# A message stage in which TensorE gathers two of every eight tiles by one-hot matrices

## The reference, cut to what matters

```python
h = jnp.maximum(_layernorm(x, axis=-1), 0.0)
edge_in = jnp.concatenate([edge_attr_64, h[src]], axis=1)    # 103125 x 128
msg = jax.nn.relu(edge_in @ W1 + b1)                         # 103125 x 64
msg_sum = jax.ops.segment_sum(msg, dst, num_segments=3125)
cnt = jax.ops.segment_sum(ones, dst, num_segments=3125)
reduced = msg_sum / jnp.maximum(cnt, 1.0)[:, None]
x = x + jax.nn.relu(jnp.concatenate([reduced, h], axis=1) @ W2 + b2)
```

## Time and profile before

| | us |
|---|---|
| median of three executions | 4684.26 |
| the profiled execution | 4702.03 |
| its span, first to last instruction | 4700.2 |
| first and last addition of the message stage (line 1640) | 3343.0 and 4599.1 |
| POOL busy / PE busy over the whole span | 1601.2 / 3335.4 |
| busy in line 1593, the gathers of this stage, 806 of them | 760.6 |

### The profile page before, as it was taken

How to read it: one execution, slowest core, us unless ns; L and a number is a source line. 1 busy time by engine, 2 the same in 40 slices (tenths; PEclk the granted TensorE clock), 3 DMA queues, 4 the chain that set the end, 5 groups by cost and what they waited for, 6 DMA issues and landing times. The chain is left out here.

```text
span 4700.2 us, 76229 instructions
## 1 busy us (share of the span) xinstructions
PE 3335.4 (71%) x17068; PEld 2240.2 (48%) x17068; DVE 1890.1 (40%) x6431; ACT 1176.8 (25%) x2939; POOL 1601.2 (34%) x1778
## 2 busy tenths in 40 slices
PE   1888787899979993777777777776455555555557
PEld 1444444455533332565566655665444444444445
DVE  4666665566620004444444444455222222222223
ACT  0566666000000001333333333343101010010100
POOL 3000000000000002566565556620366656566660
PEclk6988988899989996778777777787555555555555
DMA  0111111133367762222222222210111111111110
GB/s 26 57 59 57 59 59 59 50 105 88 115 225 286 287 230 51 56 54 54 52 54 53 53 53 54 54 45 12 34 42 44 43 43 43 42 44 42 43 43 11
DMA packets 418837, 338.43 MB, mean 72 GB/s; under 512 B 175992, under 2 KB 392088, under 8 KB 418488
## 3 DMA queue, kind: packets, MB, share of 16 engines
q1 hardware_dynamic: 362536, 277.79, 19.1%
q0 software_dynamic: 52736, 55.42, 6.0%
q10 hardware_dynamic: 3216, 0.82, 0.1%
HBM read 287.96 MB, written 45.86 MB: 71 GB/s over the span
## 5 line engine op out<-in xcount | busy, mean ns | idle before, releaser
L1593 POOL DMA_INDIRECT big<-message_table,src x806 | 760.6, 944 | 721.8 <-DVE big L1640 275.4
L1330 POOL DMA_INDIRECT big<-row_table,src x806 | 760.5, 944 | 565.1 <-issue 181.6
L1607 PE MATMUL banks<-big 64*128 64x64 f32 x1612 | 446.7, 430 | 213.2 <-DVE big L1640 196.7
L1616 PE MATMUL banks<-big 128*64 x1804 | 322.6, 328 | 384.2 <-issue 376.1
L1355 PE MATMUL banks<-big 97*128 x902 | 405.8, 541 | 153.0 <-issue 131.5
L1607 PEld LDWEIGHTS banks<-big 64*128 64x128 f32 x1612 | 373.0, 320 | 263.3 <-issue 211.5
L1371 PE MATMUL banks<-big 128*128 x1804 | 354.1, 331 | 157.7 <-ACT big L1387 105.5
L1640 DVE TENSOR_TENSOR big<-banks,big 128x128 f32<-128x128 f32 x403 | 115.7, 287 | 863.7 <-remote 776.6
L483 PE MATMUL banks<-work 128*128 128x226 f16 x1197 | 350.7, 293 | 138.3 <-issue 132.7
L1616 PEld LDWEIGHTS banks<-big 128*64 128x64 f32 x1804 | 231.1, 215 | 453.9 <-issue 418.1
L992 PE MATMUL banks<-big,work 128*64 128x512 f32 (+1 forms) x1050 | 402.0, 543 | 28.0 <-DMA big<-weights_dense 28.0
(11 more groups left out here) (280 smaller groups left out, 4897.8 us busy)
## 6 DMA issues: line engine op xcount, KB each, us to landing
big<-weights_dense SPq DMA_DIRECT2D x18, 6400.0 KB, 20.2
weights_dense<-work SPq DMA_DIRECT2D x196, 200.0 KB, 1.9
work<-weights_dense SPq DMA_DIRECT2D x196, 200.0 KB, 2.5
big<-q_table SPq DMA_DIRECT2D x451, 64.0 KB
big<-in_efT SPq DMA_DIRECT2D x403, 64.0 KB
big<-in_ea SPq DMA_DIRECT2D x403, 32.0 KB
big<-row_table,src POOLq DMA_INDIRECT x806
big<-message_table,src POOLq DMA_INDIRECT x806
```

What stands on the lines that cost most here:

```text
L1330: po.indirect_dma_start(rows[:, t % RT, s, 0:D], None, x_t.rearrange("a p c -> (a p) c"), bass.IndirectOffsetOnAxis(ap=m.src2[:, s, t:t + ...
L1593: po.indirect_dma_start(G[t % R][:, s, :], None, g_t.rearrange("a p c -> (a p) c"), bass.IndirectOffsetOnAxis(ap=m.src2[:, s, t:t + 1], ax ...
L1607: ins = pe.matmul(psM[t % 2][:, s, :], ef[t % R][:, s * P:(s + 1) * P], w_e, start=(s == 0), stop=(s == 1))
L1616: ins = pe.matmul(psA[v % 4], oh[v % 4][:, s, :], M[:, bass.ds(slot, 1), s, :].rearrange("p t c -> p (t c)"), start=(s == 0), stop=(s == 1))
```

## The change

`GP` = 8: of every group of eight tiles the last two are now gathered by PE (`on_pe`), from tile 14 on and only in full groups: 98 tiles of 403, in 49 chains. For the others POOL gathers as before; the ring `G` and the sums `T` are counted in such tiles (`pool_tiles`).

- A chain: the table stays in SBUF, scaled by a power of two and split into two float16 parts (`split`, on DVE once, after a maximum over all of it that needs a GpSimd reduction across partitions). For 512 edges, SP broadcasts their `src` to all partitions, ACT subtracts each partition's own number and writes it as float16 (line 1709). DVE compares that with each of the 25 chunks of 128 nodes (line 1781, 128 x 512 float16, ring of 32). PE multiplies each chunk of the table by the one-hot and adds up in PSUM (line 1686). The 25 are spread over eight steps, three or four to a step, ahead of the tiles that need them. ACT copies the sum out as float16 (line 1714). PE then adds it, turned and with its two parts joined, to the tile's product by two small matmuls (line 1676), and ACT takes the relu straight from PSUM and undoes the scale (line 1720). DVE's addition falls away for these tiles.
- Features: the host packs the two halves of a tile into 128 partitions x 128, and the weight is block diagonal, 128 x 128, so one matmul does what two did (lines 1679 and 1673).
- The one-hots of the destinations move from DVE to ACT: |iota - rel| for each half (line 1729), then relu(1 - that) for both (line 1735).
- In the tables stage one semaphore is merged into another.

The diff, cut to its core:

```diff
 def stage_messages(nc, m, keep, w1, ef_t, src, g_t):
...
+def on_pe(t):
+    return t >= GP and t % GP >= GP - 2 and t - t % GP + GP <= T1
...
+def chunks_of_step(i):
+    return [(q, a) for q, t in enumerate(chains()) for u in range(GP) if i == t - 3 + u for a in range(u * NCH // GP, (u + 1) * NCH // GP)]
...
+            sp.wait_ge(init, 1)
+            for h in range(2):
+                sp.dma_start(w_e[h * D:(h + 1) * D, h * D:(h + 1) * D], w1).then_inc(s_in, 16)
             for t in range(T1):
                 wait(sp, m_done, t - R + 1)
-                sp.dma_start(ef[t % R], efT[:, t * TE:(t + 1) * TE]).then_inc(m.landed_e[t % R], 16)
+                sp.dma_start(ef[t % R], ef_t[t:t + 1, :, :].rearrange("t p e -> p (t e)")).then_inc(m.landed_e[t % R], 16)
+                if t % GP == 0 and on_pe(t + 2 * GP - 2):
+                    q = chains().index(t + GP)
+                    wait(sp, key_ready, q - 1)
+                    edges = src[(t + 2 * GP - 2) * TE:(t + 2 * GP) * TE]
+                    sp.dma_start(keyI[q % 2], edges.partition_broadcast(P)).then_inc(m.landed_q[q % 2], 16)
...
+            n = 0
             for t in range(T1):
-                wait(po, added, t - R + 1)
+                if on_pe(t):
+                    continue
+                wait(po, added, n - R + 1)
                 for s in range(2):
-                    po.indirect_dma_start(G[t % R][:, s, :], None, g_t.rearrange("a p c -> (a p) c"), bass.IndirectOffsetOnAxis(
-                        ap=m.src2[:, s, t:t + 1], axis=0)).then_inc(m.landed_g[t % R], 16)
+                    po.indirect_dma_start(G[n % R][:, s, :], None, g_t.rearrange("a p c -> (a p) c"), bass.IndirectOffsetOnAxis(
+                        ap=m.src2[:, s, t:t + 1], axis=0)).then_inc(m.landed_g[n % R], 16)
+                n += 1
+                if n == 2:
+                    po.wait_ge(s_max, 1)
+                    po.partition_all_reduce(gall, gmax, P, bass.bass_isa.ReduceOp.max).then_inc(s_max, 1)
...
                     pe.wait_ge(m.landed_e[t % R], before(t) + landed(t))
-                    wait(pe, added, t - 1)
-                    for s in range(2):
-                        ins = pe.matmul(psM[t % 2][:, s, :], ef[t % R][:, s * P:(s + 1) * P], w_e, start=(s == 0), stop=(s == 1))
-                    ins.then_inc(m_done, 1)
+                    if t >= 2:
+                        if on_pe(t - 2):
+                            pe.wait_ge(m_ready, t - 1)
+                        else:
+                            pe.wait_ge(added, pool_tiles(t - 1))
+                    both = psM[t % 2].rearrange("p s c -> p (s c)")
+                    if on_pe(t):
+                        q = chains().index(t - t % GP)
+                        pe.wait_ge(h_copied, q + 1)
+                        pe.matmul(both, ef[t % R], w_s, start=True, stop=True)
+                        for s in range(2):
+                            e = (t % GP - (GP - 2)) * TE + s * P
+                            ins = pe.matmul(psM[t % 2][:, s, :], hT[q % 2][:, e:e + P], comb, start=False, stop=True, skip_group_check=True)
+                        ins.then_inc(m_done, 1)
+                    else:
+                        pe.matmul(both, ef[t % R], w_e, start=True, stop=True).then_inc(m_done, 1)
+                for q, a in chunks_of_step(i):
+                    n = q * NCH + a
+                    if a == 0:
+                        pe.wait_ge(s_max, 3)
+                        wait(pe, h_copied, q - 1)
+                    pe.wait_ge(hot_ready, n + 1)
+                    pe.matmul(psH[q % 2], table[:, a, :, :].rearrange("p s d -> p (s d)"), hot[n % HOT],
+                              start=(a == 0), stop=(a == NCH - 1)).then_inc(hot_used, 1)
...
-            for t in range(T1):
-                act.wait_ge(added, t + 1)
-                wait(act, summed, t - RT + J2)
-                nc.scalar.activation(M[:, t % RT, :, 0:D], T[t % 4], ACT.Relu).then_inc(m_ready, 1)
+            act.wait_ge(s_down, 2)
+            for i in range(-2, V2):
+                t = i
+                if t % GP == 2 and on_pe(t + GP + 4):
+                    q = chains().index(t + 6)
+                    act.wait_ge(m.landed_q[q % 2], -(-(V2 - q % 2) // R) * 16 + 16 * (q // 2 + 1))
+                    wait(act, hot_ready, NCH * (q - 1))
+                    nc.scalar.activation(key[q % 2], keyI[q % 2], ACT.Identity, bias=down).then_inc(key_ready, 1)
+                if on_pe(t + 1) and t % GP == GP - 3:
+                    q = chains().index(t - t % GP)
+                    act.wait_ge(hot_used, NCH * (q + 1))
+                    wait(act, m_done, t - 2 * GP + 3)
+                    nc.scalar.copy(hT[q % 2], psH[q % 2]).then_inc(h_copied, 1)
+                if 0 <= t < T1:
+                    wait(act, summed, t - RT + J2)
+                    if on_pe(t):
+                        act.wait_ge(m_done, t + 1)
+                        act.wait_ge(s_max, 3)
+                        ins = nc.scalar.activation(M[:, t % RT, :, 0:D], psM[t % 2], ACT.Relu, scale=m.unscale)
+                    else:
+                        act.wait_ge(added, pool_tiles(t + 1))
+                        ins = nc.scalar.activation(M[:, t % RT, :, 0:D], T[pool_tiles(t) % 4], ACT.Relu)
+                    ins.then_inc(m_ready, 1)
+                v = i + 1
+                if 0 <= v < V2:
+                    wait(act, oh_ready, v - 1)
+                    for s in range(2):
+                        ins = nc.scalar.activation(away[v % 2][:, s, :], m.iotaH[:, 0:BD], ACT.Abs, bias=m.rel2[:, s, v:v + 1], scale=-1.0)
+                    ins.then_inc(away_ready, 1)
+                v = i
+                if 0 <= v < V2:
+                    act.wait_ge(away_ready, v + 1)
+                    wait(act, summed, v - 3)
+                    nc.scalar.activation(oh[v % 4], away[v % 2], ACT.Relu, bias=1.0, scale=-1.0).then_inc(oh_ready, 1)
...
+            def split():
+                dve.wait_ge(s_max, 2)
+                dve.wait_ge(s_in, 32)
+                chain(dve.tensor_scalar(wexp, gall.bitcast(I32), 0x7F800000, None, ALU.bitwise_and))
+                chain(dve.tensor_scalar(wexp, wexp, float(87 << 23), None, ALU.max))
+                chain(dve.tensor_scalar(m.scale.bitcast(I32), wexp, -1.0, float(268 << 23), ALU.mult, ALU.add))
+                chain(dve.tensor_scalar(m.unscale.bitcast(I32), wexp, -float(14 << 23), None, ALU.add))
+                dve.tensor_scalar(w_s, w_e, m.scale, None, ALU.mult)
+                chain(dve.tensor_scalar(gt, gt, m.scale, None, ALU.mult))
+                wide = gt.rearrange("p (a d) -> p a d", a=NCH)
+                chain(dve.tensor_copy(table[:, :, 0, :], wide))
+                dve.tensor_tensor(table[:, :, 1, :], wide, table[:, :, 0, :], ALU.subtract).then_inc(s_max, 1)
...
+                if i == 3:
+                    split()
                 t = i
-                if 0 <= t < T1:
+                if 0 <= t < T1 and not on_pe(t):
+                    n = pool_tiles(t)
                     dve.wait_ge(m_done, t + 1)
-                    dve.wait_ge(m.landed_g[t % R], 2 * before(t) + landed(t, 2))
-                    wait(dve, m_ready, t - 3)
-                    dve.tensor_tensor(T[t % 4], psM[t % 2], G[t % R], ALU.add).then_inc(added, 1)
+                    dve.wait_ge(m.landed_g[n % R], 2 * before(n) + landed(n, 2))
+                    if n >= 4:
+                        dve.wait_ge(m_ready, [u for u in range(t) if not on_pe(u)][-4] + 1)
+                    dve.tensor_tensor(T[n % 4], psM[t % 2], G[n % R], ALU.add).then_inc(added, 1)
+                for q, a in chunks_of_step(i + 2):
+                    n = q * NCH + a
+                    if a == 0:
+                        dve.wait_ge(key_ready, q + 1)
+                    wait(dve, hot_used, n - HOT + 1)
+                    dve.tensor_scalar(hot[n % HOT], key[q % 2], float(P * a - CENTER), None, ALU.is_equal).then_inc(hot_ready, 1)
                 v = i - 3
                 if v >= 0:
                     dve.wait_ge(summed, v + 1)
                     wait(dve, acc_ready, v)
                     a = acc[:, bass.ds(own.of(v), 1), :].rearrange("p j c -> p (j c)")
                     dve.tensor_tensor(a, a, psA[v % 4], ALU.add).then_inc(acc_ready, 1)
...
-                v = i + 1
-                if v < V2:
-                    wait(dve, summed, v - 3)
-                    for s in range(2):
-                        ins = dve.tensor_scalar(oh[v % 4][:, s, :], m.iotaH[:, 0:BD], m.rel2[:, s, v:v + 1], None, ALU.is_equal)
-                    ins.then_inc(oh_ready, 1)
```

More of the change, by code:

```diff
@@ L1552, in _, with pool_tiles, chains, stage_messages @@
                 dve.tensor_tensor(of_group(gt, g), L[2].result(dve, g), along(b3_s, len(chunks(g))), ALU.add).then_inc(L[2].taken, 1)
-def stage_messages(nc, m, keep, w1, efT, g_t):
+GP = 8
+HOT = 32
+CENTER = NODES // 2
+def on_pe(t):
+    return t >= GP and t % GP >= GP - 2 and t - t % GP + GP <= T1
```

(26 more changed lines are left out.)

27 lines of the change are left out of this document (20 added, 7 removed).

## The result

The changed kernel takes **4427.11 us** (4419.99 to 4433.61), the kernel before on the same chip 4683.99: a ratio of 0.9454, 95% interval 0.9434 to 0.9473. The forecast was 4509, between 4370 and 4730.

The account below looks back on a forecast made before the run. The message stage was taken as bound by POOL's gather issue and PE's holes in turn. 1.89 + 0.77 = 2.66 us a tile instead of 3.125 saves 187 us, less 12 for start and tail: 4509 us, range 4370 to 4730.

Parts of the forecast that it names:

- POOL's issue and PE's holes in turn: Message stage: POOL issues a burst of gathers, then pauses while PE stands still 6.20 us; 3.11 us a tile before.
- The first term: Message stage, POOL's gather issue: 1.25 us times gathers per tile, falling from 2.50 to 1.89 us a tile.
- third rival: Message stage: DVE's comparisons keep POOL from writing gather descriptors; 5016 us, or 4762 if half shows; chance 0.14.
- upper bound of 0.69: Message stage, DVE: highest price in us of one 128x512 comparison, derived from 1.82 us for 1600 columns; 0.40 was taken.
- The second term: Message stage: POOL's pause spread over the tiles of a cycle, 2.45 p / 6.7, forecast at 0.77 us a tile.
- p: Message stage: PE's own time for a tile; 1.3 us at 2.4 GHz, 2.53 at 1.2 GHz, taken as 2.1.
- pause of 2.45: Message stage: POOL's wait in each cycle beyond its usual pitch, 2.45 us (2.76 less 0.30).
- the model: Message stage: time per tile is 1.25 x gathers per tile + 2.45 p / 6.7, forecast at 2.66 us.
- the forecast's argument for the clock: Message stage: PE, asked for more than 76%, should leave clock 0.50 as in the attention stage; 0.6 to 0.85 expected.
- second rival: Message stage: PE's windows hold fewer tiles because of 25 waits for DVE, so nothing is won; 4686 us, chance 0.14.
- Start and tail: Message stage's ends: added cost of 8 us at the start (0 to 9) and 4 at the tail (0 to 10).
- ACT and DVE: Message stage: their work stays hidden, ACT 1.3 and DVE 1.65 us a tile; DVE under 75% busy, ACT under 60%.

Follow-up runs that it names:

- plain_rows: Kernel before, with SP loading each tile's rows by one plain DMA so POOL issues nothing (gather left out): 4105.17 us, ratio 0.876.
- no_hots: Changed kernel with DVE's 128x512 comparisons done only for the first 32 blocks (later rows wrong), on the faster chip: ratio 0.9439.
- onehot_dve: Changed kernel with the destination one-hots back on DVE instead of ACT: 4432.24 us, ratio 0.9423.
- gather_only: Kernel before plus only the PE gathers for two of eight tiles; two 64-row feature products, destination one-hots on DVE: 4731.94 us, ratio 1.0063.
- gp6: Changed kernel with two tiles of every six on PE instead of two of eight: ratio 0.9406 on the faster chip, 0.9507 (4474.44 us) on another.
- sq_twice: Changed kernel with each tile's square feature product done twice in a row: 4432.61 us, ratio 0.9474.
- sq_only: Kernel before with only the square feature product (one block diagonal matmul per tile), all 806 gathers kept: 4653.39 us, ratio 0.9895.
- gp5: Changed kernel with two tiles of every five on PE instead of two of eight, on the faster chip: ratio 0.9465.

## Why the prediction was right, and where it was not

*The bound.* "POOL's issue and PE's holes in turn" held. Take the issuing away, and the stage falls to PE's own time (plain_rows); on the chip without holes it falls to POOL's issue (no_hots). So POOL's issue and PE's work are each seen alone.

*The first term.* 610 gathers at 1.25 us gave 1.89 us a tile. They stretched by 61 ns each, 0.09 a tile, 37 us in all. That is the third rival's mechanism at a small part of its price. By the Trainium skill (SBUF — State Buffer, SBUF: two separate sides) the one of DVE and GpSimd that comes second to the shared port pair "fully blocks". With 2.0 comparisons to a gather (1225 / 610) 61 ns are 30 for each, a tenth of its 287 ns, and no run shows more than a fifth in the mean. It isn't spread evenly: half of the gathers stay under 0.95 us, and a few are much longer, up to 2.16. Nor is it the comparisons alone: with the destinations' one-hots back on DVE the mean is 1051 ns in onehot_dve and 968 in gather_only, at the same 2.0. The comparison costs 0.287 us where I took 0.40. (The upper bound of 0.69 isn't what its row gives, as 1.82 x 512 / 1600 is 0.58; nothing hangs on it.)

*The second term was mis-sized, in both of its factors.* It was to be 0.77 us a tile, from p = 2.1 and a pause of 2.45. POOL's waits for an addition (us in all, times) show what it was:

```profile
  DVE big L1775: 194.0, 101
```

That is 1.92 us each, 1.62 beyond the usual 0.30, where there were 2.8; 101 x 1.62 / 402 is 0.41 us a tile. There are 402 / 101 = 3.98 tiles to a pause, about as before (4.1), so p by the model is 6.7 / 3.98 = 1.68. PE needs 1.44 us while the clock is up and 2.61 behind a hole, and the clock was 0.83 in the mean. So p was some 0.4 too large, and the pause 0.8. With the 1.90 of the issue and the gathers' 0.09 this makes 2.40 of the 2.433. 402 x (2.66 - 2.43) = 92 us is nearly all of the 100 by which the profiled execution is below its forecast of 4527. The medians show 82, since the 18 us by which the profiled execution before lay above its median did not come back after the change. Why the pause is shorter no run shows.

With p = 1.44 the model gives 1.89 + 2.45 x 1.44 / 6.7 = 2.42. That is luck: it leaves out the slow tiles and the longer gathers, and takes the pause too long. For the square product alone it gave 2.91 against 2.98, where only p was off; for gp6 2.30 against 2.55, and for sq_twice 41 us that did not come. As a rule it is not to be used.

*What the prediction did not see.* It took the square product as 0.56 us of PE's work. At 1.2 GHz it was 0.32 (1.67 against 1.35 in sq_only), and its larger part is the clock. With the old products the added matmuls leave PE full at 1.2 GHz, and the change loses (gather_only). So the forecast's argument for the clock fails. It expected the clock to move as in the attention stage once PE was asked for more, and gather_only has PE busy 300 us of 300 and stays at 0.50. The second rival, "PE takes the gain back", is what happens then, at 4731.94 by the price of 1.2 GHz and no wait for DVE. The forecast came out by luck in this step: the change held the square product too, and neither that nor the added matmuls raised the clock alone. With the rule of the Trainium skill (TensorE: Matmul & The Clock Gate, Part 1) that activity releases the clock, this trace agrees as far as the changed kernel goes; in gather_only and plain_rows PE was busy without a gap and the clock was not released, so a busy PE was not enough.

*Start and tail.* 12 us were taken. The start is seen in the fourth addition, at 3361.11, where the kernel before has it at 3350.57:

```profile
3355.28 0.29 DVE L1775 TENSOR_TENSOR big<-banks,big 128x128 f32<-128x128 f32 x1 [7.47 <-DMA big<-message_table,src]
...
3359.37 1.83 DVE L1763 TENSOR_TENSOR big<-big 128x1600 f16<-128x1600 f32 x1
3361.11 0.29 DVE L1775 TENSOR_TENSOR big<-banks,big 128x128 f32<-128x128 f32 x1
```

That is 10.5 us later, of which 1.4 are the later first addition; 9 are left, the upper bound. DVE's three passes and their small operations are 5.6 of it, and most of the rest is POOL's wait before the reduction:

```profile
L1653 POOL PARTITION_ALL_REDUCE big<-big x1 | 0.4, 377 | 6.1 <-issue 6.1
```

The reduction itself took 0.38 us, not 2.3; 6.1 us of idle time stood before it, which no row had shown. The tail cost 1.3, not 4. *ACT and DVE* were hidden, as forecast: DVE 42% and ACT 46% busy, and moving the one-hots changed nothing in the time.

## What to carry to other kernels

When work is added to TensorE at its lower clock, ask what shape the matmuls around it have: here a full PE with feature products of 64 rows stayed at 1.2 GHz, and 64 rows of zeros beside them were worth 5.6% of the whole kernel. The shape alone was not enough: with 128 rows and PE busy half of the time the clock stayed down too. Test the parts of a change together and apart: two parts that were worth +0.6% and -1.1% alone gave -5.8% together. And a time from one chip should not be set beside one from another.

## What was not expected of the hardware

- A PE busy 300 us of 300 stayed at a granted clock of 0.50 over the whole stage (gather_only, plain_rows). The same program with the feature products on 128 rows, half of them zeros, ran at 0.76. And with square products, but PE busy 148 us of 300, it was 0.50 again (sq_only).
- Chips differ by 11% on this program (4190 against 4684 to 4710), with gathers of the same length (944 to 947 ns). On the faster one PE's holes beside POOL's gathers are missing in the message stage. The attention stage is faster there too: in gp6's stretch 2200 to 2600 (below) POOL is busy 303 us of 400 and the clock 0.89, against 239 and 0.74 in the earlier trace rows. What makes the holes, and why one chip has none, stays open. The runs show that they need POOL's gathers, come with six or eight of them on end and not with pairs, and do not need PE's register work.

```profile
2200.00:2600.00 400.00, 319.80 (x1916) 258.28 (x1916) 219.61 (x1115) 190.52 (x637) 302.69 (x320) 0.89 0.33 67
```

- 16-bit comparisons of 128x512 on DVE go with longer gathers on POOL, by 30 ns per comparison in the changed kernel and 43 to 57 in gp6 and gp5. Single gathers are longer by more than one comparison of 287 ns (gp6's timeline, below, in a stage without holes); what decides which ones stays open.

```profile
3301.04 0.94 POOL L1648 DMA_INDIRECT big<-message_table,src  x1 [0.30 <-issue]
3302.29 1.46 POOL L1648 DMA_INDIRECT big<-message_table,src  x1 [0.30 <-issue]
...
3306.55 1.81 POOL L1648 DMA_INDIRECT big<-message_table,src  x1 [0.30 <-issue]
```
